# Mask terms made in the first stage, and another order of the first loads in two 16-head attention stages

## The reference

```python
# layer 1, cross attention (q = layernorm(x), k = v = ctx_1024, mask = 1 per valid key)
q, k, v = q @ wq.T + bq, k @ wk.T + bk, v @ wv.T + bv      # each split into 16 heads
scores = q k^T / sqrt(16) + (1 - mask) * -10000.0
x = x + softmax(scores) v

# layer 3, cross attention (no projections, mask per query and key)
x = x + softmax(q k^T / sqrt(16) - 1e9 * ~mask) v
```

## Time and profile before

| what | value |
|---|---|
| median of 3 runs | 2873.27 us (2872.2 to 2879.57) |
| the profiled execution | 2872.06 us, span 2870.2 us |
| PE busy / DVE busy / ACT busy / POOL busy | 2374.7 / 1862.6 / 1215.3 / 511.3 us |
| DMA | 416.39 MB, mean 145 GB/s |
| stage `l1x` begins / its first exponential | 1062.9 us / 1118.54 us |
| stage `l3x` begins / its first scores (L1653) | 2351.8 us / 2391.0 us |

### The profile page before, as it was taken

The page is one execution under the profiler, slowest core; times in us unless marked ns, Lnnn a source line. Parts: engine busy times, 40 slices in busy tenths (PEclk is TensorE's granted clock), DMA queues, the critical chain, the costliest instruction groups (busy, mean ns, idle before and its releaser), DMA issues. The chain is left out here.

```text
span 2870.2 us, 59037 instructions
## 1 busy us (share of the span) xinstructions
PE 2374.7 (83%) x22114; PEld 1475.7 (51%) x22114; DVE 1862.6 (65%) x3005; ACT 1215.3 (42%) x1871; POOL 511.3 (18%) x286
## 2 busy tenths in 40 slices
PE   3399997999995576999994869999996248999978
PEld 3344433666663463666663735555555234555547
DVE  7566666888886516666644157778885757777721
ACT  2145554333332334777772213333330225555552
POOL 0055552000000000000000016666652200000000
PEclk8699998999997796999996889999998668999989
DMA  6467785565652266767640622222221136676626
GB/s 232 170 232 249 238 273 162 154 190 162 191 161 69 76 222 146 170 151 172 155 109 25 235 83 92 90 90 90 90 90 39 54 75 159 149 153 160 153 58 236
DMA packets 255634, 416.39 MB, mean 145 GB/s; under 512 B 32177, under 2 KB 216854, under 8 KB 255354
## 3 DMA queue, kind: packets, MB, share of 16 engines
q1 hardware_dynamic: 255482, 414.17, 50.0%
HBM read 323.26 MB, written 90.85 MB: 144 GB/s over the span
## 5 line engine op out<-in xcount | busy, mean ns | idle before, releaser
L2284 PE MATMUL l2x_kf<-l2x_w,l2x_nin 128*128 128x512 f32 x784 | 341.6, 596 | 6.8 <-DMA l2x_nin<-scratch_nT 6.6
L1479 DVE CUSTOM_DVE_ANT_0 l1x_junk<-l1x_pm,l1x_mrow,l1x_top 128x896 bf16<-128x896 f32 x224 | 247.1, 1149 | 116.9 <-PE l1x_pm L1633 106.1
L1479 DVE CUSTOM_DVE_ANT_0 l3x_junk<-l3x_pm,l3x_mrow,l3x_top 128x896 bf16<-128x896 f32 x224 | 246.1, 1148 | 88.6 <-PE l3x_pm L1633 88.1
L1561 ACT ACTIVATE l1x_prob<-l1x_ring,l1x_mask_col 128x512 f32<-128x512 f32 x392 | 247.8, 684 | 115.1 <-PE l1x_ring L1653 113.9
L1564 ACT ACTIVATE l3x_prob<-l3x_ring 128x512 f32<-128x512 f32 x392 | 213.0, 595 | 161.5 <-PE l3x_ring L1657 161.5
L2284 PEld LDWEIGHTS l2x_kf<-l2x_w,l2x_nin 128*128 128x128 f32 x784 | 148.6, 191 | 191.3 <-issue 188.8
L2266 ACT ACTIVATE l2x_fsq<-l2x_f 128x1024 f32<-128x1024 f32 x98 | 103.6, 1057 | 286.7 <-DVE l2x_f L2231 286.7
L1050 ACT ACTIVATE l0x_att_pt<-l0x_att_pt 128x1024 f32<-128x1024 f32 x99 | 104.7, 1058 | 262.1 <-DVE l0x_att_pt L989 262.1
L2330 POOL TENSOR_TENSOR l2x_gk<-l2x_f,l2x_ks 128x1024 f32<-128x1024 f32 x98 | 182.3, 1896 | 159.9 <-DVEq L2256 159.9
L1094 PE MATMUL l0x_att_pv<-l0x_wv,l0x_att_vin 128*128 128x512 f32 x392 | 194.5, 619 | 1.3 <-DVE l0x_att_tops L977 1.3
L2231 DVE TENSOR_TENSOR l2x_f<-l2x_kf,l2x_bias 128x1024 f32<-128x1024 f32 x98 | 120.0, 1225 | 87.1 <-PE l2x_kf L2284 75.2
(11 more groups left out here) (690 smaller groups left out, 4733.6 us busy)
## 6 DMA issues: line engine op xcount, KB each, us to landing
l1x_kt<-scratch_KS SPq DMA_DIRECT2D x84, 448.0 KB, 9.1
l3x_kt<-scratch_KS SPq DMA_DIRECT2D x84, 448.0 KB, 9.2
scratch_KT<-l0x_max_kf SPq DMA_DIRECT2D x28, 896.0 KB, 6.8
l0x_att_kt<-scratch_KT SPq DMA_DIRECT2D x56, 448.0 KB, 7.5
scratch_KS<-l0x_side_kp SPq DMA_DIRECT2D x14, 1344.0 KB, 13.7
scratch_KS<-l2x_side_kp SPq DMA_DIRECT2D x14, 1344.0 KB, 6.0
l0f_w<-L_ffn_exp_w SPq DMA_DIRECT2D x16, 1024.0 KB, 6.3
l1f_w<-L_ffn_W SPq DMA_DIRECT2D x16, 1024.0 KB, 5.4
```

The lines of the kernel that those rows point to most:

```text
L1479: dve.tensor_tensor_reduce(junk[x % 2][:, :, :], pm[x % 2][:, :, 0:SPLIT], mrow[b][:, :].rearrange("p (s k) -> p s k", s=2), 1.0, top[1 - ...
L1561: ins = act.activation(into, scores, ACT.Exp, bias=R.mask_col[:, bass.ds(m * TILES + n // 4, 1)])
L2284: last = pe.matmul(pf[u][:, n, :], nin[b][:, c, t * P:(t + 1) * P], w[:, c, n * BANK:(n + 1) * BANK], start=(c == 0), stop=(c == DC - 1))
```

## The change

The mask terms are made in `ctx_norm` by four GpSimd instructions, from the mask as 98 rows of 128 and from a second, transposed copy of it that is laid out beforehand; the row form is stored to DRAM before the last stores of that stage. `l1x` has no mask arithmetic, no transpose of it and no wait for its store left. In both stages `lead.sync` now ends with `kt`; the loads of chunk 1, the values and (in `l1x`) wv and bv follow after `q.sync`, behind two transfers that write the rows of ones from a DRAM row.

```diff
@@ ctx_norm
+        mask = S.sb("mask", [R.keys // P, P])
+        loads = Loads(S.sem("masks"))
 ...
                 load(0, 0)
                 load(1, 0)
+                loads(sp.dma_start(mask[:, :], A["mask_row"]))
+                loads(sp.dma_start(R.mask_col[:, :], A["mask_turned"]))
 ...
+                sp.wait_ge(S.sem("mask_made"), 1)
+                sp.dma_start(R.mask_bias.rearrange("o (t p) -> (o t) p", p=P), mask[:, :]).then_inc(
+                    S.sem("mask_out"), 16)
                 for b in range(2):
                     store(b, steps - 1)
+                sp.wait_ge(S.sem("mask_out"), 16)
 ...
             def _(pool):
                 start_counts(pool, S)
+                link = Link(pool, S.sem("mask_link"))
+                pool.wait_ge(S.sem("masks"), loads.total)
+                for terms in (R.mask_col, mask):
+                    link(pool.tensor_scalar(terms[:, :], terms[:, :], -1.0, 1.0, ALU.mult, ALU.add))
+                    link(pool.tensor_scalar(terms[:, :], terms[:, :], -10000.0, None, ALU.mult))
+                pool.sem_inc(S.sem("mask_made"), 1)
@@ Heads16
-    def ones_rows(self, act):
+    def ones_rows(self, sp):
         for b in range(2):
-            act.activation(self.kt[b][STACK:STACK + 3, :, :], ... ACT.Copy, scale=0.0, bias=1.0) ...
+            sp.dma_start(self.kt[b][STACK:STACK + 3, :, :], self.R.ones_row.unsqueeze(0).broadcast_to(
+                [3, 16, CHUNK])).then_inc(self.S.sem("ones_rows"), 16)
 ...
                     lead.sync(sp)
                     q.sync(sp)
+                    self.ones_rows(sp)
+                    lead.later_sync(sp)
                     top_to_rows(0, 0)
 ...
                     if keyed:
+                        pe.wait_ge(S.sem("late_loads"), lead.late.total)
                         value_unit(0, 0, 0, ring[(N - 1) % 3]).then_inc(filled, 1)
@@ l3_xattn, Lead.sync
                     heads.load_high(sp, 0, 0)
                     heads.load_mask(sp, 0, 0)
-                    heads.later_loads(sp)
+                    heads.load_stack(sp, 0, 0)
+
+                def later_sync(self, sp):
+                    heads.load_high(sp, 0, 1)
                     heads.load_mask(sp, 0, 1)
+                    heads.load_values(sp, 0, 0)
@@ l1_xattn, Lead (the order on SyncE's queue after the change)
             def sync(self, sp):
+                loads(sp.dma_start(w[:, 0, :, :], by_rows(A["L1_xattn_wq"])))
+                loads(sp.dma_start(bq[:, :], column(A["L1_xattn_bq"]), allow_slow_non_contiguous=True))
                 loads(sp.dma_start(hm[:, :], A["c_head16"]))
                 heads.load_high(sp, 0, 0)
+                heads.load_mask(sp, 0, 0)
                 heads.load_stack(sp, 0, 0)
+
+            def later_sync(self, sp):
                 heads.load_high(sp, 0, 1)
+                heads.load_mask(sp, 0, 1)
+                self.late(sp.dma_start(w[:, 1, :, :], by_rows(A["L1_xattn_wv"])))
+                self.late(sp.dma_start(bv[:, :], A["L1_xattn_bv"].partition_broadcast(P)))
                 heads.load_values(sp, 0, 0)
```

More of the change, by code:

```diff
@@ L1330, in load_stack @@
                       self.sem(f"kt{b}"))
[L1332 to L1336, removed]
-    def ones_rows(self, act):
+    def ones_rows(self, sp):
         for b in range(2):
-            act.activation(self.kt[b][STACK:STACK + 3, :, :], self.R.ident[STACK:STACK + 3, 0:1].unsqueeze(
-                2).broadcast_to([3, 16, CHUNK]), ACT.Copy, scale=0.0, bias=1.0).then_inc(self.S.sem("ones_rows"), 1)
+            sp.dma_start(self.kt[b][STACK:STACK + 3, :, :], self.R.ones_row.unsqueeze(0).broadcast_to(
+                [3, 16, CHUNK])).then_inc(self.S.sem("ones_rows"), 16)
     def run(self, lead, q, qb, qb_turned, O, bias):
@@ L1539, in _ @@
                     if bias is not None:
+                        dve.wait_ge(S.sem("late_loads"), lead.late.total)
                         link(dve.tensor_tensor(R.x[:, :], R.x[:, :], bias[:, :], ALU.add))
@@ L1713, in _ @@
                     q.wait(pe)
-                    pe.wait_ge(S.sem("ones_rows"), 2)
+                    pe.wait_ge(S.sem("ones_rows"), 32)
                     group(0, 0, 0)
@@ L1783, in sync @@
                     heads.load_mask(sp, 0, 0)
-                    heads.later_loads(sp)
+                    heads.load_stack(sp, 0, 0)
+                def later_sync(self, sp):
+                    heads.load_high(sp, 0, 1)
                     heads.load_mask(sp, 0, 1)
+                    heads.load_values(sp, 0, 0)
                 def scalar(self, act):
                     norm_scalar(act, S, "n", nw)
-                    heads.ones_rows(act)
                 def vector(self, dve):
@@ L1831, in l1_xattn @@
     H = 16
-    n_tiles = R.keys // P
     with Stage(nc, "l1x") as S:
@@ L1840, in l1_xattn @@
         qT = S.sb("qT", [P, DC * P])
-        R.mask_col = S.sb("mask_col", [P, n_tiles])
-        R.mask_bias = nc.dram_tensor("l1x_mask_bias", (1, R.keys), F32, kind="Internal").ap()
         q_rows = [S.sb(f"q_rows{b}", [STACK + 3, 16, P], BF16) for b in range(2)]
@@ L1847, in l1_xattn, with __init__ @@
         q = QueryRows(nc, S, keep, q_rows, qT, DC)
-        mask = keep.enter_context(nc.sbuf_tensor("l1x_mask", [n_tiles, P], F32))
-        pt, pq, pm = heads.ring
+        pt, pq, _ = heads.ring
         loads = Loads(S.sem("loads"))
         class Lead:
+            def __init__(self):
+                self.late = Loads(S.sem("late_loads"))
             def sync(self, sp):
-                loads(sp.dma_start(mask[:, :], A["mask_row"]))
+                loads(sp.dma_start(w[:, 0, :, :], by_rows(A["L1_xattn_wq"])))
+                loads(sp.dma_start(bq[:, :], column(A["L1_xattn_bq"]), allow_slow_non_contiguous=True))
                 loads(sp.dma_start(hm[:, :], A["c_head16"]))
[L1857 to L1860, removed]
                 heads.load_high(sp, 0, 0)
-                sp.wait_ge(S.sem("mask_bias"), 1)
-                sp.dma_start(R.mask_bias.rearrange("o (t p) -> (o t) p", p=P), mask[:, :]).then_inc(
-                    S.sem("mask_out"), 16)
+                heads.load_mask(sp, 0, 0)
                 heads.load_stack(sp, 0, 0)
-                sp.wait_ge(S.sem("mask_out"), 16)
-                heads.load_mask(sp, 0, 0)
+            def later_sync(self, sp):
                 heads.load_high(sp, 0, 1)
+                heads.load_mask(sp, 0, 1)
+                self.late(sp.dma_start(w[:, 1, :, :], by_rows(A["L1_xattn_wv"])))
+                self.late(sp.dma_start(bv[:, :], A["L1_xattn_bv"].partition_broadcast(P)))
                 heads.load_values(sp, 0, 0)
-                heads.load_mask(sp, 0, 1)
             def scalar(self, act):
                 norm_scalar(act, S, "n", nw)
-                heads.ones_rows(act)
             def vector(self, dve):
@@ L1880, in vector @@
                 dve.wait_ge(S.sem("loads"), loads.total)
[L1881 to L1885, removed]
                 dve.wait_ge(S.sem("q_proj"), 1)
@@ L1895, in tensor @@
                 turn_tensor(pe, S, "n", xn, pt, R.ident)
-                pe.wait_ge(S.sem("mask_bias"), 1)
-                pe.transpose(pm[:, 0:n_tiles], mask[:, :], R.ident[0:n_tiles, 0:n_tiles]).then_inc(
-                    S.sem("mask_turned"), 1)
                 pe.wait_ge(S.sem("n_xT"), 1)
@@ L3302, in layout @@
     out["mask_row"] = a["mask_BxS2_ff1"].reshape(-1, P)
+    out["mask_turned"] = out["mask_row"].T
     out["mask_qk"] = a["mask_BxSxS2_bk0"][0]
@@ L3329, in program @@
         R.K1 = nc.dram_tensor("scratch_K1", (DC, P, keys), F32, kind="Internal").ap()
+        R.mask_col = sb("mask_col", [P, keys // P])
+        R.mask_bias = nc.dram_tensor("scratch_mask", (1, keys), F32, kind="Internal").ap()
         R.ones_row = nc.dram_tensor("scratch_ones", (1, CHUNK), BF16, kind="Internal").ap()
```

## The result

The changed kernel takes 2885.79 us (median of 7 runs, 2883.06 to 2888.42), the kernel before, measured alongside it as often, 2876.34: ratio 1.0035, 95% interval 1.0024 to 1.0047, that is 10 us slower (7 to 14). The forecast was 7.7 us slower.

A forecast was written before the change was run, and what follows sets the result against it. Bound by the chain from `l1x`'s 10.8 us mask-row wait to the ten units, and by `mask_bias` of chunk 1 in `l3x`. Sum 0 + 1.4 + 6.3 = 7.7 us slower; forecast 2880.5 us, range 2871 to 2888.

The forecast's parts named there:

- The two anchors: Starts that move the kernel's end: the ten units in `l1x` at 1107.66, `mask_bias` of chunk 1 in `l3x` at 2380.97.
- First stage: Added loads, mask store and four GpSimd instructions fall into idle time: cost 0, at most 1 us.
- The front of `l1x`: With the mask row ahead of `kt`, the first maximum starts at 1075.9, 12.5 us earlier.
- removing L1341 from ScalarE wins nothing: In `l1x`, L1341 (24.18 us) ends at 1088.6, before ScalarE's next work even in the earlier schedule.
- The chain on SyncE's queue: Query-part store waits behind `kt`, seen 1084.3 in `l1x` and 2370.9 in `l3x`; then twelve reads, ones and later loads.
- the rival in which it does not: Store of the query parts does not wait for `kt`, seen 2.2 us after issue: 2867.6 us; chance 5%.
- The order alone: With ones at only 0.8 us: gain of 1.5 us in `l1x`, loss of 3.1 in `l3x`.
- The price of the ones: Both transfers run on 3 of 16 engines at `kt`'s packet price, 0.136 us: 4.35 us, bounds 0.8 and 8.7.
- The upper bound of the forecast, 8.7 us: Ones at twice the `kt` packet price, as nothing shows 48 reads of one DRAM row by three engines.
- What stands behind the ones: Later loads queue behind the ones on three engines; each us above 4.35 counts twice, once in each stage.
- the fourth rival: Ones cost more than packets of `kt`, over 0.3% slower from 4.8 us on; 2889.8 at twice the price; chance 32%.
- "same": Outcome within about 0.3%, 8.6 us, the least change a measurement of this kernel can tell; chance 57%.

The follow-up runs named there:

- `f_port`: Changed kernel, but ones by ScalarE and the same two transfers into a spare tile's partitions 96, 97, 98: `mask_bias` in `l3x` 37.7 us, value projection in `l1x` 44.5.
- `h_order`: Kernel before with mask terms in the first stage, ones by ScalarE, and in `l1x` the query parts last: 2862.47 us against 2878.04, ratio 0.9945.
- `j_ones_last`: Changed kernel with the two transfers of ones behind the later loads instead of in front: ratio 1.0007 against the kernel before.
- `a_scalar`: Changed kernel, but with the rows of ones again written by ScalarE: ratio 0.9999 against the kernel before.
- `m_ports_twice`: Changed kernel, ones by ScalarE, two transfer pairs to a spare tile's partitions 0, 4, 8 and 12, 16, 20: `mask_bias` in `l3x` 37.8 us, value projection in `l1x` 44.7.
- `c_sixteen`: Changed kernel with the ones in six transfers of one partition each instead of two of three partitions: ratio 1.0027 against the kernel before.
- `b_twice`: Changed kernel with two more transfers of ones, to partitions 96 to 98 of a spare tile, behind the first two: ratio 1.0089 against the kernel before.
- `d_rows48`: Changed kernel, but each transfer of ones reads 48 different DRAM rows instead of one row 48 times: ratio 1.0046 against the kernel before.
- `g_mask_only`: Kernel before with only the mask terms made in the first stage, ones by ScalarE and loads in the old order: ratio 0.9986.

## Why the prediction was right, and where its sizes were off

**Direction and mechanism: right.** The two anchors were the right ones, and each wait that the forecast named is in the trace: TensorE for `vin`, VectorE for `mq`.

**First stage: nothing.** Its end moved from 111.1 to 111.4 us, within the 110.3 to 112.5 that the kernels with the same first stage show in single executions.

**The front of `l1x`: 12.5 us forecast, 12.7 measured.** The projection of the queries (L1904) begins 3.6 us after L124, forecast 4.1, and behind VectorE (L149) and no longer behind a load. That removing L1341 from ScalarE wins nothing is shown by `f_port`, which has it and the same transfers in the queue: first maximum at 12.7 us as in the changed kernel, V and M within 0.5. Some kernels have the first maximum at 13.5 (`h_order` with L1341, `j_ones_last` without it), so that difference of 0.9 us has another cause, which stays open.

**The chain on SyncE's queue: right to 1 us.** The 12 reads of the query rows were forecast at 21.3 and 19.1 us (1084.3 and 2370.9 less the stage's start) and begin at 21.8 and 19.2. The store of the query parts does wait behind `kt`, so the rival in which it does not is refuted.

**The order alone: right.** Without ones the forecast had a gain of 1.5 us in `l1x` and a loss of 3.1 in `l3x`; `a_scalar` shows 2.1 and 2.4.

**The price of the ones: mis-sized.** This is the term that was off: forecast 3.2 us in `l3x` and 2.9 in `l1x`, measured 6.4 and 4.3. The step that failed is "three engines at the packet price of `kt`, 0.136 us, 4.35 us". As a price of the engines it was not far off: with destinations apart three engines need 3.6 to 3.9 us for a pair (`m_ports_twice`). But the engines are not the limit: spread over 16, the pair still takes 7.0 us (`c_sixteen`). What sets it is the destination: three neighbouring partitions take 20 GB/s, 8.5 us a pair (`b_twice`). The upper bound of the forecast, 8.7 us, was there for another reason, the repeated DRAM row, and that reason fell too (`d_rows48`). The 3 small packets of the earlier trace rows were read rightly (the changed kernel's pair is 96 packets of 1792 B, and three engines raise each semaphore) and led to the wrong limit: with `kt`, no row could separate a packet's price on an engine from the price of its destination.

**What stands behind the ones: over-counted.** The forecast let everything behind them wait in full, so that each us above 4.35 counts once in each stage. The ones took 8.0 us to land in `l3x` and 7.8 in `l1x`; with 8.0 its own sum would have made them cost 6.9 and 6.6 us. Measured are 6.4 and 4.3, so in `l1x` above all a part of the other loads went on beside them. The two errors have opposite signs. That the total came out within the range is in part luck.

**The sum.** Measured at the anchors 2.2 + 8.9 = 11.1 us, against 1.4 (1.3 by the forecast's own terms, 1107.1 + 1.84 less 1107.66) + 6.3 = 7.7. Up to their ends the stages lost 1.2 and 8.2 us, so the loop of `l1x` gave about 1 us back; by ratio the kernel lost 10. That is over the 0.3% which the forecast took as the least change that can be told, if not by much (0.24 to 0.47%): the outcome is on the side of the fourth rival, the ones dearer than packets of `kt`, which with "slower" had 38%, and not on that of "same", which had 57%. In its losses this rival came true at its lower end, in the time of the ones themselves near its upper one.

## What to carry to other kernels

On a queue that is served in order, a load's place is set by what its consumer waits for, and a round trip through DRAM (here: the store behind 2.75 MB, the wait for its landing, twelve issues of 0.65 us) pushes back everything that is issued behind it: put what the first engines need ahead of it, and the round trip last. A transfer of few bytes into a few neighbouring partitions can block as long as one of a megabyte (172 KB in 8 us here, where 896 KB of `vin` took 6.5); price it by its destination, and make such rows on an idle engine or behind the loads that are waited for. Before removing what a wait seems to be for, look at what is queued ahead of it: the mask's round trip was gone in `g_mask_only`, and the wait was still 10.2 us.

## What the runs showed of the hardware

Writes to partitions 96 to 98 ran at 20 to 25 GB/s in all: 172,032 B took 8.0 us with 3 engines and rows of 1792 B, as long with rows of 28,672 B (`d_rows48`), and 7.0 with 16 engines (`c_sixteen`). To partitions 12, 16 and 20 three engines wrote the same bytes in 3.6 us, 48 GB/s, 16 GB/s each, with another load in part beside them. While such a blocked transfer is under way the DMA engines are shown as busy (share 1.10 to 1.15) at 140 GB/s: a full share is no sign of full bandwidth. Reading one DRAM row 96 times was no dearer than reading 48 rows. The time that SyncE needs to issue a transfer depends on its form: 0.82 us for two transfers to partitions 96 to 98, 1.52 for two to 0, 4 and 8, and 4.04 for six to one partition each.
